# A fused graph-attention layer: half of the last part of x loaded by a third queue

## The chip, the cores and the metric

One core of a Trainium2 chip runs the whole kernel. The metric is the device time of one execution in microseconds; three runs of the kernel before stand beside one profiled execution.

## The reference

x is 4096 x 128 in fp32, adj is 4096 x 4096 in int32 (about one entry in 256 is set, the diagonal among them), attn is 256 x 1.

```python
s_i = x @ attn[:128]
s_j = x @ attn[128:]
e = leaky_relu(s_i + s_j.T, negative_slope=0.2)
e = e + where(adj > 0, 0.0, -1e9)
alpha = softmax(e, axis=1)
out = layernorm(x + alpha @ x, axis=-1)
```

## The kernel before, in words

The 4096 rows are handled as 32 tiles of 128, eight blocks of four tiles. For each block the kernel goes over 32 chunks of neighbours. VectorE makes the weights of a chunk for the 512 rows of a block out of a row vector q, a column r and the mask (`weigh`, line 729), and TensorE multiplies them with the scaled features `xj` and adds up in PSUM (lines 877 and, for the last block, 882). adj comes in 32 pieces of 2 MB. ScalarE turns a piece to bytes (lines 421, 427), VectorE transposes the bytes to the mask (lines 613, 626). The softmax's exponentials are split into factors of row and column, which needs the largest s_j of all first; so all of x must have been read before the first weight.

How a row sits in SBUF: `x_raw` holds, for partition b of a quadrant q (32 partitions), the rows of `x` in groups of four; a load of one quadrant and a range of chunks is one DMA. x comes in three parts by chunks, `X_CUTS = [0, 8, 16, 32]`: two of 8 chunks and a last one of 16, each in four DMAs, one for each quadrant. SP issues the quadrants 0 and 1 (`LOW_HALF`), ScalarE the quadrants 2 and 3 (`HIGH_HALF`), part by part (`load_x`, line 253, with the issue in line 257). A DMA of the first two parts carries 128 KB, one of the last part 256 KB. SP issues the row of attn first (line 297). Behind x, both queues go on with the adjacency pieces (`load_piece`, line 260, issue in line 276), 512 KB for each quadrant, held by the count of pieces in flight and by free slots.

GpSimd starts with small fills: it zeroes `ident` (line 330), writes the diagonal (line 332, which gives `consts_ready`), and fills four small tiles. Later it makes `neg_last` (line 339) once all products are there, `last_x` (line 342), and small statistics of each block with the stores of the block's rows (line 356).

TensorE waits for `consts_ready`, does 14 transposes of `ident` to warm up (line 816), spreads attn over the partitions by two matmuls (lines 819, 821), and then turns x four chunks at a time (`turn_x`, line 831), with a wait for a part of x where a part begins (line 827). Between them stand the matmuls that give s_i (line 842). ScalarE copies what was turned from PSUM (line 382); after the fifth copy it sums the products of chunks 16 to 23 (line 391), which gives a quarter of s_j. VectorE copies attn (lines 579, 581), multiplies x by it in stripes of eight chunks (line 574) and sums three of the four stripes (line 570); it waits for a part of x in lines 583, 586 and 589. Then comes the maximum over s_j (line 596), its spread over the partitions by TensorE (line 858), `below_max` (line 600) and the factors on ScalarE (lines 396 to 398). VectorE then turns the first half of piece 0 (lines 631, 626) as soon as that piece has landed (line 636), and the main loop begins.

Of the kernel before, what the change touches and what calls it, by code (L numbers as in the profile page):

```python
# [14 lines left out]
def gat_kernel(nc: bass.Bass, x: bass.AP, adj: bass.AP, attn: bass.AP, out: bass.AP):  # L15
# [11 lines left out]
    Q = 4  # L27
    B = 32
    K = 4
# [7 lines left out]
    LOW_HALF = (0, 1)  # L37
    HIGH_HALF = (2, 3)
# [46 lines left out]
    X_CUTS = [0, SC, 2 * SC, CHUNKS]  # L85
    X_PARTS = len(X_CUTS) - 1
# [4 lines left out]
    x_v = x.rearrange("(q f b k) d -> q b f (k d)", q=Q, f=F, b=B, k=K)  # L91
# [3 lines left out]
    with ExitStack() as ctx:  # L95
# [3 lines left out]
        def sem(name):  # L99
            return ctx.enter_context(nc.semaphore(name))  # L100
# [61 lines left out]
        banks = [psum[:, i, :] for i in range(8)]  # L162

        x_loaded = [sem(f"x_loaded{part}") for part in range(X_PARTS)]
        attn_loaded = sem("attn_loaded")
        adj_loaded = [sem(f"adj_loaded{i}") for i in range(ADJ_SLOTS)]
        stored = sem("stored")
# [85 lines left out]
        def load_x(queue, quadrants, part):  # L253

            first, stop = X_CUTS[part], X_CUTS[part + 1]
            for q in quadrants:
                queue.dma_start(x_raw[B * q:B * (q + 1), first:stop, :].rearrange("b (f k) d -> b f (k d)", k=K),  # L257
                                x_v[q, :, first // K:stop // K, :]).then_inc(x_loaded[part], 16)

        def load_piece(queue, quadrants, g):  # L260

            if g >= IN_FLIGHT:
                landed = g - IN_FLIGHT
                queue.wait_ge(adj_loaded[landed % ADJ_SLOTS], 16 * Q * (landed // ADJ_SLOTS + 1))
            if g == PROD_SLOT:
                queue.wait_ge(row_max_ready, 1)
            elif g == XT_SLOT:
                queue.wait_ge(s_i_in_psum, RB)
            elif ADJ_SLOTS <= g < ADJ_SLOTS + BY_DVE:
                queue.wait_ge(half_bytes_ready, 1)  # L270
                queue.wait_ge(first_bytes_ready, g - ADJ_SLOTS + 1)
            elif g >= ADJ_SLOTS + BY_DVE:
                queue.wait_ge(bytes_ready, g - ADJ_SLOTS - BY_DVE + 1)
            n, p = ORDER[g]
            for q in quadrants:
                queue.dma_start(adj_in[B * q:B * (q + 1), g % ADJ_SLOTS, :, :, :],  # L276
                                adj_v[n, p, q, :, :, :, :]).then_inc(adj_loaded[g % ADJ_SLOTS], 16)
# [16 lines left out]
        @block.sync  # L294
        def _(sp):

            sp.dma_start(attn_row_in[:], attn[:, :].rearrange("d o -> o d")).then_inc(attn_loaded, 16)
            for part in range(X_PARTS):
                load_x(sp, LOW_HALF, part)
            for g in range(ALL_PIECES):  # L300
                load_piece(sp, LOW_HALF, g)


            for g in range(EARLY):
                sp.wait_ge(early_out_ready, g + 1)
                for q in LOW_HALF:
                    store_last(sp, g, q, last_stored)
            for g in range(EARLY, len(FINAL_GROUPS)):
                sp.wait_ge(last_out_ready, g - EARLY + 1)
                for q in LOW_HALF:  # L310
                    store_last(sp, g, q, last_stored)


            sp.wait_ge(again_ready, 1)
            with sp.If(sp.value_load(again[0:1, 0:1], min_val=0, max_val=1) > 0):
                sp.wait_ge(stored, 16 * Q * NORM_GROUPS)
                sp.wait_ge(early_stored, 16 * len(HIGH_HALF) * EARLY)
                sp.wait_ge(last_stored, 16 * (Q * len(FINAL_GROUPS) - len(HIGH_HALF) * EARLY))
                sp.dma_start(xi[:], xi_v).then_inc(inputs_again, 16)
                sp.dma_start(attn_col, attn[D:2 * D, :]).then_inc(inputs_again, 16)  # L320
                sp.dma_start(attn_row, attn[0:D, :].rearrange("d o -> o d").broadcast_to([P, D])).then_inc(inputs_again, 16)
                with sp.Fori(0, TILES) as t:
                    sp.wait_ge(adj_rows_free, t + 1)
                    sp.dma_start(adj_rows, adj[bass.ds(t * P, P), :]).then_inc(adj_rows_loaded, 16)
            sp.wait_ge(early_stored, 16 * len(HIGH_HALF) * EARLY)
            sp.wait_ge(last_stored, 16 * (Q * len(FINAL_GROUPS) - len(HIGH_HALF) * EARLY))

        @block.gpsimd
        def _(pool):
            nc.gpsimd.memset(ident[:], 0.0).then_inc(ident_zeroed, 1)  # L330
            pool.wait_ge(ident_zeroed, 1)
            nc.gpsimd.affine_select(out=ident[:], in_=ident[:], compare_op=ALU.not_equal, fill=1.0, base=0,
                                    pattern=[[-1, P]], channel_multiplier=1).then_inc(consts_ready, 1)
            nc.gpsimd.memset(half[:], -0.5)
            nc.gpsimd.memset(eps[:], EPS)
            nc.gpsimd.memset(rden[:], 0.0)
            nc.gpsimd.memset(worst[:], 0.0).then_inc(worst_ready, 1)
            pool.wait_ge(products_ready, STRIPES)
            nc.gpsimd.tensor_scalar(neg_last[:], x_raw[:, :, DEN], -1.0, 0.0, ALU.mult, ALU.add).then_inc(neg_last_ready, 1)
            pool.wait_ge(neg_last_ready, 1)  # L340
            pool.wait_ge(factors_ready, 1)
            nc.gpsimd.tensor_tensor(last_x[:], neg_last[:], d_j[:], ALU.mult).then_inc(last_x_ready, 1)  # L342

            for g in range(NORM_GROUPS):

                pool.wait_ge(total_ready, g + 1)
                nc.gpsimd.tensor_scalar(neg_mean[:, 0:K], total[:, 0:K], -1.0 / D, 0.0, ALU.mult, ALU.add).then_inc(mean_ready, 1)  # L347
                pool.wait_ge(squares_ready, g + 1)
                nc.gpsimd.tensor_scalar(variance[:, 0:K], square_sum[:, 0:K], 1.0 / D, EPS, ALU.mult, ALU.add).then_inc(variance_ready, 1)
                pool.wait_ge(variance_ready, g + 1)  # L350
                nc.gpsimd.tensor_tensor(rstd[:, 0:K], variance[:, 0:K], half[:, 0:K], ALU.pow).then_inc(rstd_ready, 1)  # L351
                pool.wait_ge(rstd_ready, g + 1)
                nc.gpsimd.tensor_tensor(offset[:, 0:K], neg_mean[:, 0:K], rstd[:, 0:K], ALU.mult).then_inc(offset_ready, 1)  # L353
                pool.wait_ge(out_ready, g + 1)
                for q in range(Q):
                    pool.dma_start(out_v[g, q, :, :],  # L356
                                   x_raw[B * q:B * (q + 1), g * K:(g + 1) * K, :].rearrange("b k d -> b (k d)")).then_inc(stored, 16)

            for g, v in enumerate(FINAL_GROUPS[:EARLY]):
                pool.wait_ge(moments_ready, v.stop)  # L360
                nc.gpsimd.tensor_scalar(variance[:, v], moments[:, v, 1], 1.0, EPS,
                                        ALU.mult, ALU.add)
                nc.gpsimd.tensor_scalar(neg_mean[:, v], moments[:, v, 0], -1.0, 0.0,
                                        ALU.mult, ALU.add).then_inc(variance_ready, 1)
                pool.wait_ge(variance_ready, NORM_GROUPS + g + 1)
                nc.gpsimd.tensor_tensor(rstd[:, v], variance[:, v], half[:, v], ALU.pow).then_inc(rstd_ready, 1)
                pool.wait_ge(rstd_ready, NORM_GROUPS + g + 1)
                nc.gpsimd.tensor_tensor(offset[:, v], neg_mean[:, v], rstd[:, v], ALU.mult).then_inc(offset_ready, 1)
            for g in range(EARLY):
                pool.wait_ge(early_out_ready, g + 1)  # L370
                for q in HIGH_HALF:
                    store_last(pool, g, q, early_stored)

        @block.scalar
        def _(act):

            for part in range(X_PARTS):
                load_x(act, HIGH_HALF, part)
            load_piece(act, HIGH_HALF, 0)
            for m in range(RB):  # L380
                act.wait_ge(xT_in_psum, m + 1)
# [183 lines left out]
        def _(dve):  # L565
# [20 lines left out]
            dve.wait_ge(x_loaded[1], 16 * Q)  # L586
            product_of(1)
            sum_products(1)
            dve.wait_ge(x_loaded[2], 16 * Q)
            product_of(2)  # L590
            product_of(3)
            sum_products(3)
# [220 lines left out]
        def _(pe):  # L813
# [10 lines left out]
            def turn_x(m):  # L824

                if m * K in X_CUTS:
                    pe.wait_ge(x_loaded[X_CUTS.index(m * K)], 16 * Q)
                if m >= 4:
                    pe.wait_ge(xT_ready, m - 3)
                for k in range(K):  # L830
                    last = nc.tensor.transpose(banks[XT_BANK + m % 4][:, k * P:(k + 1) * P], x_raw[:, m * K + k, :], ident[:])  # L831
                last.then_inc(xT_in_psum, 1)
# [156 lines left out]
```

## Time and profile before

| | |
|---|---|
| three runs, us | 252.92, 252.38, 252.85; median 252.85 |
| the profiled execution, us | 252.96 |
| its span, us | 251.2 |
| mean granted TensorE clock of the span | 0.992 |
| TensorE busy | 241.8 us (96%) |
| VectorE busy | 233.2 us (93%) |
| ScalarE busy | 175.8 us (70%) |
| GpSimd busy | 36.3 us (14%) |
| moved by DMA | 71.50 MB, mean 285 GB/s |

The span is the time from the first to the last instruction that the profile shows; the execution's own time is 1.8 us more. A row of the page's slices has 40 digits of 6.3 us each, every one a busy share in tenths. Busy time of an engine is not the path that sets the end: which wait ends last must be read from the chain and the timeline. In the rows, SPq, ACTq and POOLq are the queues of SyncE, ScalarE and GpSimd at work on an issue, PE is TensorE's matmul and PEld its weight load.

### The profile page before, as it was taken

To read this page: it belongs to the slowest core of one execution; us is meant where nothing else is said; L and a number is where in the kernel's file an instruction comes from. 1 tells how busy PE (TensorE), PEld (TensorE's weight loads), DVE (VectorE), ACT (ScalarE), POOL (GpSimd) and SP (SyncE) were. 2 spreads that over 40 slices of the span, in tenths; PEclk is the share of its full clock that TensorE was granted. 3 is DMA by queue.
4 is the path that set the end of the run, shared out by engine and by line. 5 is a ranking of instruction groups with operands and counts; after the bars stand their busy time and mean duration, and the time that the engine had idled before them with its cause. 6 is when DMAs were issued, how large, how long until landed. Compare 5 with 4: busy or idle time off the path is not lost.

```text
span 251.2 us, 2777 instructions
## 1 busy us (share of the span) xinstructions
PE 241.8 (96%) x801; PEld 127.4 (51%) x801; DVE 233.2 (93%) x383; ACT 175.8 (70%) x257; POOL 36.3 (14%) x74
## 2 busy tenths in 40 slices
PE   7799999999999999999999999999999999999991
PEld 6453344444444444444444444444444444799991
DVE  1879899999999999999999999999999999999834
ACT  0589988889886387995996569876996659404402
POOL 1010000000000034330150003300330004301612
PEclk9799999999999999999999999999999999999999
DMA  7999999999999999999999999999999990100101
GB/s 196 310 348 348 349 349 348 348 348 348 348 348 349 347 348 349 312 355 348 348 350 363 348 349 348 348 363 348 350 347 362 347 267 23 46 0 1 25 19 44
DMA packets 70258, 71.50 MB, mean 285 GB/s; under 512 B 2881, under 2 KB 68738, under 8 KB 70242
## 3 DMA queue, kind: packets, MB, share of 16 engines
q1 hardware_dynamic: 34690, 34.74, 44.1%
q10 hardware_dynamic: 34592, 34.67, 44.1%
q0 software_dynamic: 960, 1.90, 2.5%
q8 instruction: 7, 0.11, 0.2%
q14 instruction: 9, 0.07, 0.1%
HBM read 69.21 MB, written 2.10 MB: 284 GB/s over the span
## 4 chain that ended last, share of the span: by engine, by line
PE 89%; ACT 3%; DMA 2%; DVE 2%; ACTq 1%; SPq 1%; issue 1%; POOL 0%; DVEq 0%; POOLq 0%
PE psum L877 74%; PE psum L882 11%; DMA x_raw<-in_x_dram 2%; ACT mask_bytes L421 1%; PE psum L871 1%; PE psum L842 1%; PE psum L831 1%; ACT xj L409 1%; ACT adj_in L391 1%; ACTq L276 1%; SPq L257 0%; POOL last_x L342 0%; DVE weights L729 0%; DVE mask_t L626 0%; ACT adj_in L382 0%
## 5 line engine op out<-in xcount | busy, mean ns | idle before, releaser
L877 PE MATMUL psum<-weights,xj 128*128 128x512 f32 x448 | 194.0, 593 | 0.7 <-DVE weights L729 0.6
L729 DVE SCALAR_TENSOR_TENSOR weights<-q_row,r_j,mask_t 128x512 f32<-128x512 f32 x256 | 172.2, 741 | 0.4
L877 PEld LDWEIGHTS psum<-weights,xj 128*128 128x128 f32 x448 | 84.2, 190 | 106.1 <-issue 82.6
L427 ACT ACTIVATE mask_bytes<-adj_in 128x4096 uint8<-128x4096 int32 x27 | 97.5, 3613 | 29.5 <-DMA adj_in<-in_adj_dram 26.6
L613 DVE STREAM_TRANSPOSE mask_t<-mask_bytes 128x1024 uint32<-128x1024 uint32 x27 | 33.4, 1237 | 0.0
L882 PEld LDWEIGHTS psum<-xj,weights 128*128 128x128 f32 x256 | 28.8, 192 | 0.5 <-issue 0.5
L882 PE MATMUL psum<-xj,weights 128*128 128x128 f32 x256 | 28.9, 275 | 0.0
L347 POOL TENSOR_SCALAR neg_mean<-total 128x4 f32<-128x4 f32 x7 | 2.2, 311 | 154.3 <-ACT x_raw L440 154.2
L421 ACT ACTIVATE mask_bytes<-adj_in 128x2048 uint8<-128x2048 int32 x9 | 16.7, 1898 | 1.5 <-DMA adj_in<-in_adj_dram 1.5
L356 POOL DMA_DIRECT2D out_dram<-x_raw x28 | 14.6, 525 | 19.8 <-ACT x_raw L454 19.7
L440 ACT ACTIVATE x_raw<-x_raw 128x128 f32<-128x128 f32 x28 | 8.2, 294 | 11.1 <-DVE x_raw L672 11.1
L447 ACT ACTIVATE unused<-x_raw,neg_mean 128x128 f32<-128x128 f32 x28 | 10.9, 390 | 4.4 <-POOL neg_mean L347 4.4
L409 ACT ACTIVATE xj<-x_raw,last_x,d_j 128x127 f32<-128x127 f32 x32 | 13.2, 480 | 0.5 <-POOL last_x L342 0.3
L454 ACT ACTIVATE x_raw<-x_raw,offset,rstd 128x128 f32<-128x128 f32 x28 | 11.5, 479 | 2.6 <-POOL offset L353 2.6
L351 POOL TENSOR_TENSOR rstd<-variance,half 128x4 f32<-128x4 f32 x7 | 9.6, 1368 | 0.6
L672 DVE SCALAR_TENSOR_TENSOR x_raw<-psum,rden,x_raw 128x127 f32<-128x127 f32 x32 | 9.2, 343 | 0.4
L842 PE MATMUL psum<-adj_in,attn_iw 128*128 128x512 f32 x16 | 8.5, 657 | 0.0
L626 DVE STREAM_TRANSPOSE mask_t<-mask_bytes 128x512 uint32<-128x512 uint32 x10 | 7.1, 706 | 0.8 <-ACT mask_bytes L421 0.8
L382 ACT COPY adj_in<-psum 128x512 f32<-128x512 f32 x8 | 4.4, 582 | 3.7 <-PE psum L831 3.7
L831 PE MATMUL psum<-ident,x_raw 128*128 128x128 f32 x32 | 5.0, 310 | 1.7 <-DMA x_raw<-in_x_dram 1.7
L435 ACT COPY sums<-psum 128x512 f32<-128x512 f32 x7 | 4.1, 580 | 3.7 <-PE psum L877 3.7
L517 ACT ACTIVATE deviations<-moments,eps 128x1 f32<-128x1 f32 x2 | 0.6, 294 | 8.5 <-DVE moments L696 8.5
(65 smaller groups left out, 77.2 us busy)
## 6 DMA issues: line engine op xcount, KB each, us to landing
adj_in<-in_adj_dram ACTq DMA_DIRECT2D x64, 512.0 KB, 12.7
adj_in<-in_adj_dram SPq DMA_DIRECT2D x64, 512.0 KB, 13.3
out_dram<-x_raw POOLq DMA_DIRECT2D x28, 64.0 KB, 5.3
x_raw<-in_x_dram ACTq DMA_DIRECT2D x4, 128.0 KB, 3.2
x_raw<-in_x_dram SPq DMA_DIRECT2D x4, 128.0 KB, 3.4
x_raw<-in_x_dram ACTq DMA_DIRECT2D x2, 256.0 KB, 6.0
x_raw<-in_x_dram SPq DMA_DIRECT2D x2, 256.0 KB, 7.0
out_dram<-x_raw SPq DMA_DIRECT2D x2, 32.0 KB, 1.5
```

Source lines behind the costliest of these rows:

```text
L351: nc.gpsimd.tensor_tensor(rstd[:, 0:K], variance[:, 0:K], half[:, 0:K], ALU.pow).then_inc(rstd_ready, 1)
L356: pool.dma_start(out_v[g, q, :, :], x_raw[B * q:B * (q + 1), g * K:(g + 1) * K, :].rearrange("b k d -> b (k d)")).then_inc(stored, 16)
L409: nc.scalar.activation(xj[:, c, 0:DEN], x_raw[:, c, 0:DEN], ACT.Identity, bias=last_x[:, c:c + 1], scale=d_j[:, c:c + 1]).then_inc(xj_scal ...
L421: half_bytes = nc.scalar.activation(mask_bytes[:, g % BYTE_SLOTS, :, :, part], adj_in[:, g % ADJ_SLOTS, :, :, part], ACT.Sign)
L427: nc.scalar.activation(mask_bytes[:, g % BYTE_SLOTS, :, :, :], adj_in[:, g % ADJ_SLOTS, :, :, :], ACT.Sign).then_inc(bytes_ready, 1)
L447: last = nc.scalar.activation(unused[:, k, :], tile(g * K + k), ACT.Square, bias=neg_mean[:, k:k + 1], accum_out=square_sum[:, k:k + 1])
L454: last = nc.scalar.activation(tile(g * K + k), tile(g * K + k), ACT.Identity, bias=offset[:, k:k + 1], scale=rstd[:, k:k + 1])
L613: nc.vector.transpose(dst.rearrange("p f (r a) -> p r f a", a=B), src).then_inc(mask_ready, 1)
L729: nc.vector.scalar_tensor_tensor(weights[:, slot_of(g * PC + j), :], q_row[:, n * BANK:(n + 1) * BANK], r_j[:, c:c + 1], mask_t[:, g % MAS ...
L842: nc.tensor.matmul(banks[bank][:, :], attn_iw[:], xT[:, rb * BANK:(rb + 1) * BANK], start=True, stop=True).then_inc(s_i_in_psum, 1)
L877: nc.tensor.matmul(banks[SUM_BANK[n % 2]][:, :], xj[:, c, :], weights[:, slot_of(g * PC + j), :], start=(c == 0), stop=(c == CHUNKS - 1)). ...
L882: return nc.tensor.matmul(banks[((BLOCKS - 1) * K + t) % 8][:, 0:D], weights[:, slot, t * P:(t + 1) * P], xj[:, c, :], start=(c == 0), sto ...
```

## The change

The last part of x is split by queue. GpSimd issues the quadrants 1 and 3 before all else that it does; SP issues quadrant 0, ScalarE quadrant 2. GpSimd's two DMAs count on a semaphore of their own, and TensorE and VectorE wait for both semaphores where they waited for one.

```diff
         x_loaded = [sem(f"x_loaded{part}") for part in range(X_PARTS)]
+        last_x_loaded = sem("last_x_loaded")
...
+        def load_last_x(queue, quadrants):
+
+            first, stop = X_CUTS[-2], X_CUTS[-1]
+            for q in quadrants:
+                queue.dma_start(x_raw[B * q:B * (q + 1), first:stop, :].rearrange("b (f k) d -> b f (k d)", k=K),
+                                x_v[q, :, first // K:stop // K, :]).then_inc(last_x_loaded, 16)
...
         @block.sync
...
-            for part in range(X_PARTS):
+            for part in range(X_PARTS - 1):
                 load_x(sp, LOW_HALF, part)
+            load_x(sp, LOW_HALF[0:1], X_PARTS - 1)
...
         @block.gpsimd
         def _(pool):
+            load_last_x(pool, (LOW_HALF[1], HIGH_HALF[1]))
             nc.gpsimd.memset(ident[:], 0.0).then_inc(ident_zeroed, 1)
...
         @block.scalar
...
-            for part in range(X_PARTS):
+            for part in range(X_PARTS - 1):
                 load_x(act, HIGH_HALF, part)
+            load_x(act, HIGH_HALF[0:1], X_PARTS - 1)
...
-            dve.wait_ge(x_loaded[2], 16 * Q)
+            dve.wait_ge(x_loaded[2], 16 * Q // 2)
+            dve.wait_ge(last_x_loaded, 16 * Q // 2)
             product_of(2)
...
                 if m * K in X_CUTS:
-                    pe.wait_ge(x_loaded[X_CUTS.index(m * K)], 16 * Q)
+                    part = X_CUTS.index(m * K)
+                    pe.wait_ge(x_loaded[part], 16 * Q if part < X_PARTS - 1 else 16 * Q // 2)
+                    if part == X_PARTS - 1:
+                        pe.wait_ge(last_x_loaded, 16 * Q // 2)
```

## Rows read from the trace of the kernel before

**Rows 1.** The page's slices of the span: busy tenths in 40 slices.

```profile
PE   7799999999999999999999999999999999999991
DMA  7999999999999999999999999999999990100101
```

**Rows 2.** The chain of waits in order of time: start us, us, what.

```profile
2.47 5.76 DMA x_raw<-in_x_dram
...
10.15 2.61 PE psum L842 x4
...
28.27 47.64 PE psum L877 x110
...
223.42 22.35 PE psum L882 x200
```

**Rows 3.** Line 257's issues (ns min/median/max), and us to landing of those at 3.5 us.

```profile
L257 ACTq DMA_DIRECT2D x_raw<-in_x_dram x6: 408/448/453, 0.7 to 3.1; - x6
L257 SPq DMA_DIRECT2D x_raw<-in_x_dram x6: 352/427/432, 1.1 to 3.4; - x6
...
x_raw<-in_x_dram SPq DMA_DIRECT2D x1, 256.0 KB, 8.1
```

**Rows 4.** The timeline from 0 to 32 us: start us, us, engine, line, [idle before].

```profile
1.53 3.25 PE L816 MATMUL psum<-ident 128*128 128x128 f32 x14 [1.53 <-POOL ident L332]
5.78 1.22 DVE L574 TENSOR_TENSOR adj_in<-x_raw,attn_j 128x1024 f32<-128x1024 f32 x1
8.27 1.88 PE L831 MATMUL psum<-ident,x_raw 128*128 128x128 f32 x8 [1.71 <-DMA x_raw<-in_x_dram]
11.49 2.36 DVE L574 TENSOR_TENSOR adj_in<-x_raw,attn_j 128x1024 f32<-128x1024 f32 x2 [0.76 <-DMA x_raw<-in_x_dram]
12.60 1.04 PE L831 MATMUL psum<-ident,x_raw 128*128 128x128 f32 x8
13.24 0.59 ACT L382 COPY adj_in<-psum 128x512 f32<-128x512 f32 x1 [1.97 <-PE psum L831]
13.47 1.02 PE L842 MATMUL psum<-adj_in,attn_iw 128*128 128x512 f32 x2
13.88 1.22 DVE L570 TENSOR_REDUCE s_j<-adj_in 128x8 f32<-128x1024 f32 x1
16.27 0.19 DVE L596 TENSOR_REDUCE smax<-s_j 128x1 f32<-128x32 f32 x1 [1.16 <-ACT adj_in L391]
17.51 0.15 DVE L601 TENSOR_SCALAR smax<-smax 128x1 f32<-128x1 f32 x1
17.58 1.23 DVE L631 TENSOR_SCALAR mask_bytes<-adj_in 128x2048 uint8<-128x2048 int32 x1
20.52 7.15 PE L877 MATMUL psum<-weights,xj 128*128 128x512 f32 x16
28.27 1.12 PE L877 MATMUL psum<-weights,xj 128*128 128x512 f32 x2 [0.60 <-DVE weights L729]
```

**Rows 5.** Line 276's issue at 4.7 us and its landing; stages (last three: PEclk, DMA share, GB/s).

```profile
L276 SPq DMA_DIRECT2D adj_in<-in_adj_dram x1: 2023/2023/2023, 4.7 to 4.7; - x1
adj_in<-in_adj_dram SPq DMA_DIRECT2D x1, 512.0 KB, 12.9
...
2.00:10.00 8.00, 6.29 (x35) 5.60 (x34) 4.58 (x6) 2.94 (x4) 0.00 (x0) 0.90 1.01 279
8.00:12.00 4.00, 3.73 (x11) 2.62 (x12) 3.21 (x4) 1.52 (x3) 0.00 (x0) 0.57 1.08 312
12.00:28.00 16.00, 15.33 (x48) 6.96 (x46) 13.09 (x20) 14.25 (x36) 1.13 (x2) 1.00 1.10 348
```

**Rows 6.** GpSimd's stores: issue ns min/median/max, and us to landing at 98, 236, 247 us.

```profile
L356 POOL DMA_DIRECT2D out_dram<-x_raw x28: 496/496/725, 98.0 to 237.9; - x28
L284 POOL DMA_DIRECT2D out_dram<-x_raw x2: 498/546/593, 246.7 to 247.3; - x2
...
out_dram<-x_raw POOLq DMA_DIRECT2D x4, 64.0 KB, 5.6
out_dram<-x_raw POOLq DMA_DIRECT2D x4, 64.0 KB, 1.9
```

## The prediction

> **What bounds the kernel now.** I read the page from the top. Its shares and slices [rows 1] show TensorE busy in every slice but the first, last and second; DMA is full from slice 2 to slice 32 and then falls off. So after the start TensorE sets the pace. The chain of waits says the same: from 28.27 us it is matmuls of lines 877 and 882 without a gap to 245.76 us [rows 2], that is 217.5 us in which the loads are always ahead. The chain's foot in time order [rows 2] is where x matters: SP's issues, a 5.76 us transfer of x that lands at 8.23, eight transposes, four matmuls of s_i, four more transposes (line 831, up to 13.21), a copy on ScalarE, sixteen steps of the sums of line 391, and then the maximum over s_j. Nothing behind 28.3 us depends on x, so this change can only move the whole block from there on earlier or later: what happens before the first product (20.52 us, [rows 4]) is all there is to win or lose.
>
> The transfer on that chain is the second part of x, not the last one. It lands at 8.23; TensorE had stood idle 1.71 us for it [rows 4]. The last part, which the change touches, was issued last on SP at 3.4 us and took 8.1 us to land [rows 3], thus 11.5 us. One engine waited for it: VectorE, 0.76 us before line 574 [rows 4]. TensorE was then still at its matmuls of line 842 and asked for the last part only at 12.6. What VectorE makes of the last part has slack too: its product is there at 12.7 (half of the 2.36 us from 11.49), while ScalarE begins line 391 at 13.72; and the last reduction ends at 15.10, while the maximum of line 596 waited 1.16 us longer, for ScalarE, and began at 16.27 [rows 4]. So the last part could land **1.0 us later or any amount earlier and the start would not notice**.
>
> There is a second thing to see at the end of the start-up. VectorE turns the first half of adjacency piece 0 at 17.58 (line 631), right behind its line 601 [rows 4]. SP's second quadrant of that piece was issued at 4.7 and took 12.9 us [rows 5]: 17.6 us. Both conditions come together within 0.1 us. A faster x alone therefore brings the first product no earlier; the adjacency piece has to land earlier as well.
>
> **The change part by part.**
> - Removed from SP and ScalarE: one issue each, 0.43 and 0.45 us at the median [rows 3]. All that stands behind them on their queues comes forward by that: the adjacency issues (SP from 3.89, ScalarE from 3.57) and ScalarE's table load and copies from 5.98. The copies then wait for TensorE or TensorE for x, so I cost this at nothing. The issues coming forward do not by themselves bring bytes forward, because the queues have work waiting from 2 us on.
> - Added on GpSimd: two issues ahead of the fill of ident. The 28 stores of line 356 cost 496 ns at the median and 725 ns at most [rows 6]; 1.0 to 1.5 us together. They move four times fewer rows each (32 runs of 2 KB against 128), so if the price went by rows it would be 4 x 0.5 x 2 = 4.0 us. I take 1.1: the stores of 32 KB cost as much as those of 64 KB [rows 6], which speaks for a fixed price. Behind them wait ident, consts_ready, and with it TensorE's 14 warm-up transposes (from 1.53, 3.25 us long), the matmul of line 819 and VectorE's attn_j. So VectorE's first product moves from 5.78 to about 6.9 and it is through with the first part at 9.4 in place of 8.25. That costs nothing: VectorE has the 0.76 us before the last part's product, and 1.16 us before line 596, 1.9 us in all [rows 4].
> - Moved: 2 x 262 kB = 524 kB of x now run at the very start on a third queue, **beside the first two parts instead of behind them**. From 2 to 10 us the core moved 279 GB/s [rows 5], and the DMA engines show 1.01 of their time busy: they have nothing free. 524 kB at 279 GB/s is 1.9 us. If GpSimd's bytes all go ahead of the end of part 1, it lands 1.9 us later; that is the upper bound. It is reached if the three queues share equally, as SP and ScalarE then have 1,049 kB to move for the first two parts and GpSimd 524 kB, so that all end together. The lower bound is 0: under load a store of GpSimd took 5.6 us to land and without load 1.9 [rows 6], so its bytes may come too late to be in the way. The stores of an idle system are nearer to the first microseconds than the stores of a full one, so I take two thirds of the upper bound, **1.2 us**: part 1 lands at 9.45.
> - The last part: SP and ScalarE still bring its other half, behind the first two parts. Bytes ahead of it are the same as before, so about 11.5 us, with 1.0 us of slack. Nothing gained.
> - The chain behind part 1: 8.27 to 13.24 at line 382, no slack in it, and each step of it to 20.52 follows from the one before. +1.2 us. VectorE with part 1 at 9.45 does 1.23 + 1.22 + 2.36 + 1.22 us, and ends at 15.5, ahead of the maximum at 17.5: not the bound.
> - Adjacency piece 0: SP has 524 - 262 kB of x less ahead of it, GpSimd 524 kB more beside both. The total to be moved is unchanged: 17.6 us again, no longer the last to come.
>
> Sum: 0 + 0 + 1.2 = +1.2 us on the span of 251.2 and on the profiled execution's own 252.96 us, which is 0.1 above the median of 252.85. From the median: 254.05; I say **254.0**.
>
> On the shared engines there is a rule to set beside this. The row [rows 5] shows 279 GB/s while x loads and 348 once only adjacency rows run. Were the gap due to having just two queues, a third one would fill it: 2,097 kB of x at 348 is 1.5 us less than at 279, and the sum would become about -0.3. The Trainium skill (DMA: Bandwidth & Descriptors, Issuing engines are not separate DMA queues) says that DMAs of all issuing engines run on the same engines and interleave, and that another issuer saves only the issue time; by that rule nothing of the 1.5 us comes and +1.2 stands.
>
> **The rivals.**
> - *TensorE's clock.* The granted clock is 0.57 of full from 8 to 12 us [rows 5], that is the lower level of 1.2 GHz for most of it, after 1.71 us of idling [rows 4]; it costs the chain: eight transposes take 1.88 us there and 1.04 at the full clock, four matmuls of line 842 take 2.61 against 2 x 1.02 [rows 2, 4], 1.4 us in all. With the warm-up moved 1.1 us later and part 0 landing later too, TensorE's work comes closer to part 1 and the idle gap is about as long as now (9.45 less some 7.9, 1.6 us) or shorter. If the clock stays at the upper level, the delay of 1.2 is paid back: -0.2 us by TensorE, but piece 0 holds VectorE at 17.6, so 0.0: 252.9. For it: the work before the gap is later and denser. Against it: the gap itself is hardly smaller.
> - *Faster.* The third queue fills the 279 GB/s, or GpSimd's rows come late enough to leave part 1 alone while SP and ScalarE reach the adjacency 0.45 us sooner, and the clock holds. Then the chain is 0.5 to 1 us earlier, and the 0.6 us that TensorE waited for weights at 28.27 [rows 4] shrinks with ScalarE being early: 252.1. Against it: the engines' busy share of about 1 and the piece that lands at 17.6.
> - *GpSimd's issues are dear.* At 2 us each consts_ready comes 4 us later, VectorE's first product at 9.8, its last reduction at 9.8 + 2 x 2.45 + 2.36 + 1.22 = 18.3 in place of 15.1, 2.0 us after the maximum's 16.27: 254.9. This decides from 1.9 us of delay on. The 725 ns at most of [rows 6] speak against it.
>
> **How the numbers follow.** Part 1 delayed and the clock as now: 0.48. Clock held, near zero: 0.22. Faster: 0.22. Dear issues: 0.08. This kernel's three runs span 0.2% (0.5 us), about what a measurement can tell from no change. Of the first case, with a delay anywhere from 0 to 1.9 us, some 0.06 falls within 0.5 us, of the clock case a part to each side. Faster by over 0.2%: 0.24; within: 0.27; slower: 0.49. Range: from the rival's 252.1 to the upper bound 252.85 + 1.9 and a half of the dear case on top, 255.2.
>
> **What would show it.** Right: part 1's transfer on the chain lands at 9 to 10 us in place of 8.23; TensorE's idle before line 831 ends there; line 382 at 14 to 15; the first product at 21.5 to 22; the block from there to the end as long as before. GpSimd's two issues 0.5 to 0.75 us each, the warm-up starting at 2.6. Wrong: part 1 landing by 8.5, a granted clock of 1.0 from 8 to 12 us, or GB/s over 300 from 2 to 10 us; and a first product before 20.5 would need piece 0 before 17.5.

## The result, and the profile after

The changed kernel takes 253.4 us (median of 19 runs, 252.67 to 254.34) against 252.4 for the kernel before (19 runs, 251.79 to 253.55). The ratio is 1.0044, with a 95% interval of 1.0033 to 1.0054: **slower by 1.1 us** (0.8 to 1.4). The forecast was +1.2 us. The ratios here and below leave out one execution, of experiment 2's kernel, that took 261.8 us in a slower state of the chip.

The profiled execution took 253.41 us, its span is 251.6. Its slices of the page answer to [rows 1]:

```profile
PE   4999999999999999999999999999999999999991
DMA  7999999999999999999999999999999990100101
```

From the third slice on nothing has changed; the first slice of TensorE has gone from 7 to 4 tenths. The chain of waits in order of time, in the stretch that answers to [rows 2]:

```profile
2.48 7.33 DMA x_raw<-in_x_dram
...
9.86 1.65 PE psum L846 x8
11.51 1.72 PE psum L857 x4
13.23 0.45 PE psum L846 x4
```

The transfer of part 1 lands at 9.81 us in place of 8.23, 1.6 us later. What follows it is shorter than before: eight transposes, four matmuls and four transposes take 3.8 us where they took 4.9. The timeline of the same kernel shows where each engine stands (lines 828, 846, 857 are those that were 816, 831, 842; line 585 was 574, 393 was 382, 608 was 596, 643 was 631, 892 was 877):

```profile
1.32 1.25 POOL L265 DMA_DIRECT2D x_raw<-in_x_dram  x2 [0.88 <-POOLq L994]
2.57 0.22 POOL L340 MEMSET ident<- 128x128 f32 x1
3.38 3.25 PE L828 MATMUL psum<-ident 128*128 128x128 f32 x14 [3.38 <-POOL ident L342]
7.71 1.97 PE L846 MATMUL psum<-ident,x_raw 128*128 128x128 f32 x8
8.02 1.22 DVE L585 TENSOR_TENSOR adj_in<-x_raw,attn_j 128x1024 f32<-128x1024 f32 x1
9.86 1.65 PE L846 MATMUL psum<-ident,x_raw 128*128 128x128 f32 x8 [0.18 <-DMA x_raw<-in_x_dram]
12.79 2.35 DVE L585 TENSOR_TENSOR adj_in<-x_raw,attn_j 128x1024 f32<-128x1024 f32 x2
13.70 0.59 ACT L393 COPY adj_in<-psum 128x512 f32<-128x512 f32 x1 [1.48 <-PE psum L846]
16.73 0.19 DVE L608 TENSOR_REDUCE smax<-s_j 128x1 f32<-128x32 f32 x1 [0.33 <-ACT adj_in L402]
18.04 1.22 DVE L643 TENSOR_SCALAR mask_bytes<-adj_in 128x2048 uint8<-128x2048 int32 x1
20.97 7.16 PE L892 MATMUL psum<-weights,xj 128*128 128x512 f32 x16
```

The row of the kernel before that shows GpSimd's first fill:

```profile
0.73 0.21 POOL L330 MEMSET ident<- 128x128 f32 x1 [0.29 <-POOLq L979]
```

Beside this row and [rows 4]: GpSimd's two issues occupy it to 2.57, the warm-up starts at 3.38 in place of 1.53 (1.85 us later), TensorE begins part 0 at 7.71 in place of about 5.5 and is done with it at 9.68. It then waits only 0.18 us for part 1, where the kernel before waited 1.71. **Two delays end at the same point**: TensorE is ready at 9.7, part 1 has landed at 9.8. VectorE's first product has moved from 5.78 to 8.02, and VectorE works nearly without a break from there; its wait before the maximum has shrunk from 1.16 to 0.33 us. The first matmul of the main loop comes at 20.97 in place of 20.52. From there to the end of the span the kernels take the same, 230.7 us before (251.2 less 20.52) and 230.6 after (251.6 less 20.97), so the whole difference lies ahead of it.

GpSimd's issues, and two stages of the changed kernel (columns as in [rows 5]):

```profile
L265 POOL DMA_DIRECT2D x_raw<-in_x_dram x2: 566/632/697, 1.3 to 2.0; - x2
...
2.00:10.00 8.00, 6.44 (x27) 5.49 (x28) 2.44 (x4) 2.15 (x3) 1.25 (x8) 1.00 1.03 267
8.00:12.00 4.00, 3.82 (x18) 3.15 (x17) 3.93 (x5) 2.12 (x4) 0.00 (x0) 1.00 1.08 317
```

An issue costs 0.57 and 0.70 us. From 2 to 10 us the core moves 267 GB/s, with 279 before [rows 5]. The profiles of all these kernels scatter from 267 to 288 there, with two queues and with three, so the third queue brings no bytes that two did not. The Trainium skill's rule (DMA: Bandwidth & Descriptors, Issuing engines are not separate DMA queues), that all issuers share the same engines and another one saves only issue time, agrees with this row.

The two profiles show +0.4 us of span where the medians show +1.0. The profiled execution of before was one of its slower ones (252.96 us, with a median of 252.4), and a rare one: its mean granted clock was 0.992, and of 75 other executions of the same kernel with a clock on record three were as low (253.0 to 253.3 us). So the experiments are read by their ratios, and the traces for the mechanism.

### The profile page after: what moved, and what is told of

Same layout as the page of the kernel before. It is cut to its first block, busy times and chain, and to the rows that moved or that the text cites. A ratio compares the mean times of both kernels' runs of the same rounds, so it can differ in the third digit from the quotient of the medians.

```text
span 251.6 us, 2778 instructions
## 1 busy us (share of the span) xinstructions
PE 242.0 (96%) x801; PEld 127.8 (51%) x801; DVE 233.2 (93%) x383; ACT 175.9 (70%) x257; POOL 38.1 (15%) x76
## 4 chain that ended last, share of the span: by engine, by line
PE 88%; ACT 3%; DMA 3%; DVE 2%; ACTq 1%; SPq 1%; issue 1%; POOL 0%; DVEq 0%; POOLq 0%
PE psum L892 74%; PE psum L897 11%; DMA x_raw<-in_x_dram 3%; ACT mask_bytes L432 1%; PE psum L886 1%; PE psum L846 1%; ACTq L284 1%; ACT adj_in L402 1%; PE psum L857 1%; ACT xj L420 1%; SPq L258 0%; POOL last_x L352 0%; DVE weights L741 0%; DVE mask_t L638 0%; ACT adj_in L393 0%
## 5 line engine op out<-in xcount | busy, mean ns | idle before, releaser
L357 POOL TENSOR_SCALAR neg_mean<-total 128x4 f32<-128x4 f32 x7 | 3.0, 430 | 153.5 <-ACT x_raw L451 153.4
L857 PE MATMUL psum<-adj_in,attn_iw 128*128 128x512 f32 x16 | 7.5, 594 | 0.0
L828 PE MATMUL psum<-ident 128*128 128x128 f32 x14 | 3.2, 425 | 3.4 <-POOL ident L342 3.4
```

The source lines that it names most:

```text
L857: nc.tensor.matmul(banks[bank][:, :], attn_iw[:], xT[:, rb * BANK:(rb + 1) * BANK], start=True, stop=True).then_inc(s_i_in_psum, 1)
```

## The experiments

Two causes were on the table. D: the 524 kB that run early displace part 1 of x. I: the two issues hold back ident, the warm-up and all that waits for attn. Each kernel below was timed against the kernel before on the same chip. "+1.6 us" is what the ratio is above 1, times 252.4 us. A trace shows one execution, which need not be a typical one. The diffs show the main lines of each edit; some leave out the waits and semaphores that go with them.

**1. The changed kernel with the issues behind the fill of ident** (bytes still early, nothing held back).

```diff
-            load_last_x(pool, (LOW_HALF[1], HIGH_HALF[1]))
             nc.gpsimd.memset(ident[:], 0.0).then_inc(ident_zeroed, 1)
...
                                     pattern=[[-1, P]], channel_multiplier=1).then_inc(consts_ready, 1)
+            load_last_x(pool, (LOW_HALF[1], HIGH_HALF[1]))
```

> The changed kernel with GpSimd's two issues moved behind the fill of ident. Two causes are to be told apart. D: the moved bytes run ahead of part 1 of x, which lands late. I: the two issues hold back ident, and with it the warm-up, so TensorE reaches part 1 late whatever the transfer does. D expects the warm-up at 1.5 us again, but part 1 still at 9.5 to 10 us with TensorE idle for over 2 us before it, and a time 1.0 to 1.8 us above the kernel before. I expects a time within 0.3 us of the kernel before.

Measured: 254.1 us, ratio 1.0062 (1.0040 to 1.0085), +1.6 us (1.0 to 2.1). Its timeline, a piece of its chain, and its stage from 8 to 12 us:

```profile
1.53 3.25 PE L828 MATMUL psum<-ident 128*128 128x128 f32 x14 [1.53 <-POOL ident L341]
9.42 1.97 PE L846 MATMUL psum<-ident,x_raw 128*128 128x128 f32 x8 [2.86 <-DMA x_raw<-in_x_dram]
11.18 3.62 PE L857 MATMUL psum<-adj_in,attn_iw 128*128 128x512 f32 x4
...
15.55 0.59 ACT adj_in L393
...
8.00:12.00 4.00, 2.58 (x9) 2.10 (x10) 2.81 (x4) 1.16 (x2) 0.00 (x0) 0.55 1.07 333
```

As D expected: the warm-up is back at 1.53, part 1 lands at 9.4, just under the 9.5 expected, and TensorE idles 2.86 us before it. The bytes alone make the kernel slower. The clock is granted at 0.55 of full behind the gap, so the steps from part 1 to ScalarE's fifth copy take 6.1 us, with 3.8 in the changed kernel. This trace is of one of the longer executions (255.1 us): its mean granted clock of 0.981 is shared by four of the twelve, the four longest (254.6 to 255.3), while the other eight have 0.993 or more. The steps of those eight are not shown.

**2. The issues without the bytes** (the kernel before, and two small DMAs of as many pieces ahead of the fill).

```diff
+        scratch = sb("scratch", [P, K * 16], fp32)
...
         def _(pool):
+            for q in (1, 3):
+                pool.dma_start(scratch[B * q:B * (q + 1), :].rearrange("b (f w) -> b f w", w=16),
+                               x_v[q, :, SC * 2 // K:CHUNKS // K, 0:16]).then_inc(scratch_loaded, 16)
             nc.gpsimd.memset(ident[:], 0.0).then_inc(ident_zeroed, 1)
```

> The kernel before, with two DMAs of 8 KB each (128 pieces of 64 bytes, the same count of pieces as the moved ones) issued by GpSimd as its first act into a scratch tile; x comes by SP and ScalarE as before. D expects no change (within 0.3 us), part 1 at 8.2 us. I expects the warm-up at 3.4 us, TensorE ready for part 1 only at 9.6 to 9.7 us and 0.6 to 1.2 us above the kernel before.

Measured: 253.44 us, ratio 1.0037 (1.0018 to 1.0056), +0.9 us (0.5 to 1.4). The issues' line, the chain of waits, and ScalarE's first sum in the timeline:

```profile
L333 POOL DMA_DIRECT2D scratch<-in_x_dram x2: 564/630/695, 1.3 to 2.0; - x2
...
1.32 1.25 POOL scratch L333 x2
...
3.38 3.14 PE psum L822 x14
...
7.40 1.23 DVE adj_in L580
8.65 1.22 DVE s_j L576
...
13.42 0.31 ACT L397 ACTIVATE adj_in<-adj_in 128x128 f32<-128x128 f32 x1 [1.20 <-DVE adj_in L580]
```

As I expected in time, and so D is not the only cause. The issues cost what they cost with 32 times the bytes (8 KB here, 256 KB there). But the chain does not run as expected: it goes through GpSimd, the warm-up, attn_j and then VectorE's products and sums one after another, not through TensorE's turn of part 1 (it turned parts 0 and 1 without a wait, done at 9.05); ScalarE waits 1.20 us for VectorE's product before its sums. The trace is of the fastest of the executions (252.62 us), so it shows the path and not the size.

**3. The changed kernel with the same bytes first, by SP and ScalarE** (no third queue, no hold-up).

```diff
+            load_last_x(sp, LOW_HALF[1:2])
             for part in range(X_PARTS - 1):
                 load_x(sp, LOW_HALF, part)
...
-            load_last_x(pool, (LOW_HALF[1], HIGH_HALF[1]))
...
+            load_last_x(act, HIGH_HALF[1:2])
             for part in range(X_PARTS - 1):
                 load_x(act, HIGH_HALF, part)
```

> The changed kernel without GpSimd's part: SP and ScalarE issue the same two quadrants of the last part ahead of parts 0 and 1. Nothing holds GpSimd back, and the same 524 kB stand ahead of parts 0 and 1, all of them. D expects part 1 at 10 us or later (8.23 plus 1.9) and 1.5 to 2.5 us above the kernel before. I expects no change within 0.3 us.

Measured: 253.68 us, ratio 1.0052 (1.0030 to 1.0075), +1.3 us (0.8 to 1.9), somewhat under D's range. Its timeline:

```profile
7.24 3.68 PE L847 MATMUL psum<-ident,x_raw 128*128 128x128 f32 x16 [1.31 <-DMA x_raw<-in_x_dram]
```

The order of the bytes costs this without any third queue. The wait has moved to part 0, which lands at 7.2, with 4.9 before; part 1 landed at 8.8, ahead of TensorE, which had turned part 0 at about 9.1, and not at 10 as expected.

**4. The changed kernel with the third queue only behind part 0** (GpSimd fills, waits for part 0, then issues).

```diff
-            load_last_x(pool, (LOW_HALF[1], HIGH_HALF[1]))
...
             nc.gpsimd.memset(worst[:], 0.0).then_inc(worst_ready, 1)
+            pool.wait_ge(x_loaded[0], 16 * Q)
+            load_last_x(pool, (LOW_HALF[1], HIGH_HALF[1]))
```

> GpSimd fills first, waits until part 0 has landed and only then issues its half of the last part: third queue, but neither held back nor ahead of part 0. D expects part 1 at 8.2 to 8.9 us and 0 to 0.4 us above the kernel before. I expects no change. If GpSimd's half lands behind 12.6 us, a third cause sets in, the last part itself, and the time is above by what it is late.

Measured: 257.44 us, ratio 1.0195 (1.0163 to 1.0228), +4.9 us. TensorE's turn of part 1 and line 586 of VectorE in the timeline, and GpSimd's issues at 5.3 us with their time to landing:

```profile
6.80 1.09 PE L847 MATMUL psum<-ident,x_raw 128*128 128x128 f32 x8 [0.18 <-DMA x_raw<-in_x_dram]
15.80 2.36 DVE L586 TENSOR_TENSOR adj_in<-x_raw,attn_j 128x1024 f32<-128x1024 f32 x2 [5.11 <-DMA x_raw<-in_x_dram]
...
x_raw<-in_x_dram POOLq DMA_DIRECT2D x2, 256.0 KB, 9.4
```

The third cause named in the expectation: now the last part itself is late, at 15.8 us, and VectorE waits 5.11 us for it. Issued at the start, GpSimd's DMAs landed in 6.0 us (median of the two); issued among running ones, in 9.4. The time says nothing on D, but the landing of part 1 does: with the 524 kB behind it instead of beside it, it lands at 6.8 us, the earliest of all traces and under what D expected.

**5. The kernel before, profiled a second time.**

> The kernel before, unchanged, for a second look at where part 1 of x lands and what clock the chain behind it gets. If the landing at 8.23 us of the first look is a fixed property of the order of the bytes, it is 8.0 to 8.5 again; if it scatters, it is elsewhere between 6.5 and 8.5 us.

Measured: 252.32 us, span 250.5. Its timeline:

```profile
5.85 3.59 PE L831 MATMUL psum<-ident,x_raw 128*128 128x128 f32 x16
6.17 1.22 DVE L574 TENSOR_TENSOR adj_in<-x_raw,attn_j 128x1024 f32<-128x1024 f32 x1
9.28 1.88 PE L842 MATMUL psum<-adj_in,attn_iw 128*128 128x512 f32 x4
14.74 0.19 DVE L596 TENSOR_REDUCE smax<-s_j 128x1 f32<-128x32 f32 x1 [0.19 <-ACT adj_in L391]
16.35 1.23 DVE L631 TENSOR_SCALAR mask_bytes<-adj_in 128x2048 uint8<-128x2048 int32 x1 [0.22 <-DMA adj_in<-in_adj_dram]
19.29 7.15 PE L877 MATMUL psum<-weights,xj 128*128 128x512 f32 x16 [0.38 <-ACT xj L409]
```

It scatters. SP's last quadrant of part 1 took 4.7 us to land here and 5.8 in the first profile, from the same issue at 2.47, and so part 1 was there at 7.2. TensorE does not wait for it, and the maximum comes at 14.74 in place of 16.27. The granted clock reads 1.00 from 8 to 12 us, but the durations say more: the sixteen transposes from 5.85 take 3.59 us, mostly at the pace of the lower level, and the four matmuls from 9.28 take 1.88, that of the upper one. In the first profile the order was the reverse, with the lower level behind the gap and the upper one ahead of it:

```profile
5.47 1.10 PE L831 MATMUL psum<-ident,x_raw 128*128 128x128 f32 x8
```

VectorE runs from 6.17 to that maximum with hardly a break: **in this execution VectorE has no slack**. That fits what the hold-up of experiment 2 costs: its maximum came at 15.97, 1.2 us behind this one.

One more thing comes out when the landings of part 1 are put side by side. In the five traces where no bytes of the last part run ahead of it or beside it (the two of the kernel before, experiments 2, 4 and 6) it lands at 8.2, 7.2, 7.2, 6.8 and 7.2 us. In the five with all 524 kB ahead or beside (the changed kernel, experiments 1, 3, 7 and 8) it lands at 9.8, 9.4, 8.8, 9.7 and 8.9. The groups do not overlap and their means lie 2.0 us apart. The first profile of the kernel before has the latest landing of its group.

**6. The gap of the kernel before filled with 12 transposes.**

```diff
             for m in range(4):
+                if m == 2:
+                    for _ in range(12):
+                        nc.tensor.transpose(banks[WARM_BANK][:, 0:P], ident[:], ident[:])
                 turn_x(m)
```

> The kernel before with 12 more transposes of ident (1.6 us at the upper clock) in the gap of TensorE before part 1. If the lower clock behind the gap costs the chain, its granted clock from 8 to 12 us becomes 1.0, the fifth copy on ScalarE comes at 12 us in place of 13.2 and the median falls by 0.3 to 0.8 us (adjacency piece 0, at 17.6 us, holds the rest). If the gap has nothing to do with the median, no change, or up to 0.3 us slower where the fillers run at the lower clock and end behind part 1.

Measured: 252.73 us, ratio 1.0015 (1.0001 to 1.0030): no gain, if anything 0.4 us slower. The clock held (granted 1.00 from 8 to 12 us, four matmuls in 1.88), but in this trace VectorE then waited 0.85 us for adjacency piece 0 in line 631, TensorE waited 1.00 us for ScalarE's xj, and the first product came at 19.87. The gap is no lasting loss of the kernel before: experiment 5 shows an execution without any.

**7. Experiment 1 with its gap filled by 20 transposes** (the loop of experiment 6, with 20 in place of 12).

> The changed kernel with GpSimd's issues behind the fill of ident and 20 more transposes in the gap of TensorE before part 1 (2.6 us of the 2.86 seen). If the 1.6 us that the unfilled one lost are 1.2 for the later landing and the rest for the lower clock, this one is 0.3 to 1.0 us above the kernel before; if they are the landing alone, 1.6 above as without the fillers.

Measured: 252.66 us, ratio 1.0032 (1.0014 to 1.0051), +0.8 us (0.4 to 1.3), half of what experiment 1 lost. The ratio is further from 1 than the median shows, because the twelve executions fall into two groups, seven from 252.2 to 252.7 and five from 253.2 to 254.5. The timeline, of one in the lower group:

```profile
6.52 2.35 PE L863 MATMUL psum<-ident 128*128 128x128 f32 x20
9.74 1.09 PE L846 MATMUL psum<-ident,x_raw 128*128 128x128 f32 x8 [0.88 <-DMA x_raw<-in_x_dram]
10.67 1.88 PE L857 MATMUL psum<-adj_in,attn_iw 128*128 128x512 f32 x4
```

Part 1 lands at 9.7, as late as ever, and the steps behind it run at the upper clock: 1.88 us for the four matmuls, 3.62 in experiment 1. Of the 1.6 us there, about half is the later landing and half what filling the gap gives back. That is an estimate by the middle of two wide intervals (1.0 to 2.1 and 0.4 to 1.3), which overlap.

**8. The changed kernel with 6 warm-up transposes in place of 14** (`WARM = 6`).

> The changed kernel with 6 in place of 14 warm-up transposes: TensorE is done with part 0 some 1.9 us earlier and waits for part 1. If the two delays end at the same point (TensorE ready at 9.7, part 1 landed at 9.8), taking away one of them gains nothing: within 0.4 us of the changed kernel, so 0.7 to 1.5 us above the kernel before. If the held-back warm-up alone is the cause, it gains most of the 1.1 us.

Measured: 254.94 us, ratio 1.0110 (1.0093 to 1.0127), +2.8 us, 1.7 more than the changed kernel. Both expectations missed. Its timeline:

```profile
3.38 1.54 PE L828 MATMUL psum<-ident 128*128 128x128 f32 x6 [3.38 <-POOL ident L342]
8.93 1.97 PE L846 MATMUL psum<-ident,x_raw 128*128 128x128 f32 x8 [0.84 <-DMA x_raw<-in_x_dram]
10.69 3.62 PE L857 MATMUL psum<-adj_in,attn_iw 128*128 128x512 f32 x4
```

TensorE is ready sooner and waits for part 1, as said. But it stays at the pace of the lower level: the four matmuls take 3.62 us, with 1.88 in the changed kernel, and the maximum waits 3.10 us for ScalarE. So the edit took away a delay and also the work that stood ahead of the wait, and the test of "two delays end at the same point" is not a clean one. What the experiments do show is that the delays don't add up: the issues alone cost 0.5 to 1.4 us, the bytes alone 1.0 to 2.1, which is 1.5 at the least, and both together 0.8 to 1.4. The timelines offer a reason, which no run isolates: in the changed kernel TensorE is at work nearly up to the landing and its four matmuls run at the upper level, where the bytes alone leave a gap of 2.86 us and the lower level behind it. That both together cost less than the bytes alone is not shown, since those intervals overlap.

**9. The changed kernel with one quadrant in place of two as GpSimd's first act** (the waits count accordingly).

```diff
-            load_last_x(pool, (LOW_HALF[1], HIGH_HALF[1]))
+            load_last_x(pool, LOW_HALF[1:2])
...
-            load_x(act, HIGH_HALF[0:1], X_PARTS - 1)
+            load_x(act, HIGH_HALF, X_PARTS - 1)
```

> The changed kernel with one quadrant (262 kB of SP's) on GpSimd as its first act in place of two. Hold-up of the warm-up and bytes ahead of part 1 are both about half: warm-up at 2.7 to 2.8 us, part 1 at 8.7 to 9.1. By these two causes 0.4 to 0.8 us above the kernel before.

Measured: 252.7 us, ratio 1.0014 (1.0000 to 1.0028), +0.4 us. The warm-up starts at 2.83; part 1 was there at 8.0, earlier than expected and within what the kernel before shows. In this trace ScalarE waits 1.14 us for VectorE's product, as in experiment 2. Less of the change costs less, as both causes have it; the run does not tell them apart.

**10. The kernel before with one quadrant of part 1 on the third queue, behind the fill** (the waits count accordingly).

```diff
-            for part in range(X_PARTS):
-                load_x(sp, LOW_HALF, part)
+            load_x(sp, LOW_HALF, 0)
+            load_x(sp, LOW_HALF[0:1], 1)
+            load_x(sp, LOW_HALF, 2)
...
                                     pattern=[[-1, P]], channel_multiplier=1).then_inc(consts_ready, 1)
+            pool.dma_start(x_raw[B:2 * B, SC:2 * SC, :].rearrange("b (f k) d -> b f (k d)", k=K),
+                           x_v[1, :, SC // K:2 * SC // K, :]).then_inc(pool_x_loaded, 16)
```

> The kernel before, where GpSimd, behind the fill of ident, issues one quadrant of part 1 (128 KB of SP's) in place of SP. The third queue now carries bytes that are wanted next, and nothing is put ahead of parts 0 and 1. If the order of the bytes is what made the changed kernel slow, part 1 lands no later than in the two looks at the kernel before (8.2 us at most) and the time is 0.5 us below to 0.2 above it. If the third queue itself costs, part 1 lands at 8.5 us or later and the time is over 0.4 us above.

Measured: 252.21 us, ratio 0.9990 (0.9975 to 1.0006): no difference that can be told from the kernel before. Its timeline:

```profile
1.76 0.68 POOL L336 DMA_DIRECT2D x_raw<-in_x_dram  x1 [0.29 <-issue]
8.14 1.97 PE L839 MATMUL psum<-ident,x_raw 128*128 128x128 f32 x8 [0.32 <-DMA x_raw<-in_x_dram]
```

Part 1 lands at 8.1, between the two profiles of the kernel before, though later than in four of the five traces of the first group. A third queue costs no time that can be measured here, where it carries the bytes that are wanted next and is issued behind the fill; it gains nothing either. No kernel that was tried beats the one before beyond its interval.

## Why the prediction was right, and where not

The sign, the place and the size were right: +1.2 us forecast, +1.1 (0.8 to 1.4) measured, all of it before the first product. The steps under it fared differently, and that the sum came out so close is in part luck.

- *The bytes displace part 1*: right in kind, and put too low. 1.2 us were taken out of bounds of 0 and 1.9, by two landings of stores. The two first profiles show 1.6 us (9.81 against 8.23), and the two groups of five landings 2.0, about the upper bound. Alone it costs +1.6 us (experiment 1). Experiment 3 shows that it is the order and not the queue.
- *GpSimd's issues cost nothing*: **the step that failed.** Their size was well put (1.1 us against 1.25), but GpSimd began them only at 1.32, where ident's fill had begun at 0.73, so the hold-up of the warm-up was 1.85 us, and VectorE's first product came 2.2 us later (8.02 against 5.78) and not 1.1. That alone is over the 1.9 us of slack that the prediction counted. And that slack was read from one profile, in which the lower clock held TensorE and ScalarE back. In experiment 5 the slack is gone, and the issues alone cost +0.9 us (experiment 2), where the sum has 0.
- *The chain behind part 1 stays as long*: wrong in the changed kernel, 3.8 us in place of 4.9. The rival on the clock had this, and expected it to pay back the whole delay; it pays back part. A granted clock of 1.0 from 8 to 12 us was named as a sign of being wrong, and it came (1.00). The misses, costs left out and a relief left out, cancelled.
- *The last part and piece 0 are no bound*: right for the changed kernel (VectorE takes the last part at 12.79 without a wait, line 643 follows the maximum's steps at once). In faster starts VectorE did wait for piece 0 (0.22, 0.85 and 0.33 us in experiments 5, 6 and 10). TensorE's own wait before the first product was then for ScalarE's xj (0.38, 1.00 and 0.48), so that piece 0 sets the start there is not shown.
- *The issues are dear, 2 us each* and *the third queue fills the gap to 348 GB/s*: both fell, by 0.57 to 0.70 us per issue and by 267 GB/s.
- The first product was expected at 21.5 to 22 us and came at 20.97, the fifth copy at 14 to 15 and came at 13.70. The +1.1 us is not to be had from two profiles: the start of the kernel before alone scatters by as much (20.52 and 19.29).
- The forecast time of 254.0 us was 0.6 too high, mostly because it started from a median of three runs, 252.85; that of nineteen is 252.4.

What stays open: why SP's quadrant of part 1 lands at 7.2 in one execution and 8.2 in another, and why TensorE, with the same warm-up at the same time, turns part 0 at the upper level in one and at the lower in the other. The experiments did not go after either.

## What to carry to other kernels

Before moving a load to the head of another queue, ask which load it will run beside: the bytes ahead of the next wait count, not the issue time saved. Here the DMA engines were full (busy share about 1), and 524 kB that came forward put the next 1 MB back by some 2 us. A cost that is "covered by slack" needs the slack of every engine that waits behind the moved instruction, and from more than one profile where the start depends on clock and landing. Two delays that end at the same point don't add up, so undoing one of them may gain nothing: experiments 1 and 8 each undid one, and neither kernel came out faster than the changed one.

## What was not expected of the hardware

- An issue by GpSimd took the same 0.56 to 0.70 us for 128 pieces of 2 KB and for 128 of 64 bytes; the stores' 32 pieces took 0.50 [rows 6]. As first act it started at 1.32 us, a memset in its place at 0.73.
- A GpSimd load issued at 5.3 us, among running transfers, took 9.0 to 9.7 us to land, with 4.7 to 7.4 for the one issued at 1.3.
- The granted clock reads 1.00 in the first 8 us of the traces, yet 14 transposes of the warm-up take 3.25 us in most of them (0.23 each) and eight of x at 7.71 in the changed kernel take 1.97, as eight do behind the gap of experiment 1, where the clock is granted at 0.55; at the upper level eight take 1.04 to 1.10. In experiment 8 the row still reads 1.00 from 8 to 12 us, while the four matmuls take 3.62 us, as they do in experiment 1 at 0.55. So at the start of these traces the durations tell the level and the row does not; where it falls behind a gap, as in the first profile of the kernel before, the durations agree with it.
